# A state-space scan between attention and feed-forward: its pieces ordered anew on four engines

## What is computed

```python
dt = softplus(dt_unproj @ W_dt.T + b_dt)        # params = x @ W_params.T
u  = silu(causal_conv(x @ W_x.T))
A_tilde = exp(dt[..., None] * A);  B_tilde = (A_tilde - 1) / A
h = A_t * h + B_t * Bp_t[:, None, :] * u_t[:, :, None]   # 16 states for each feature
y_t = einsum('bn,bdn->bd', Cp_t, h)
y = (y + u * D_param) * silu(z);  return y @ W_out.T
```

## Time and profile before

| | |
|---|---|
| median of 3 runs | 1992.88 us (1989.69 to 1998.08) |
| profiled execution | 1992.94 us, span 1991.2 us, mean granted TensorE clock 0.970 |
| busy, page part 1 | PE 1885.0 us (95%), DVE 1611.4 (81%), ACT 1100.8 (55%), POOL 682.3 (34%) |
| the scan | 1208.2 to 1762.3 us |
| attention | 168 to 918 us |

### The profile page before, as it was taken

How to read it: one execution, slowest core, us unless ns; L and a number is a source line. 1 busy time by engine, 2 the same in 40 slices (tenths; PEclk the granted TensorE clock), 3 DMA queues, 4 the chain that set the end, 5 groups by cost and what they waited for, 6 DMA issues and landing times. The chain is left out here.

```text
span 1991.2 us, 26035 instructions
## 1 busy us (share of the span) xinstructions
PE 1885.0 (95%) x7526; PEld 845.0 (42%) x7526; DVE 1611.4 (81%) x2582; ACT 1100.8 (55%) x1526; POOL 682.3 (34%) x467
## 2 busy tenths in 40 slices
PE   8989999999999999999999997899999999699998
PEld 4532332332322323324676663343344344256666
DVE  6888998998999989985556658999998999954655
ACT  5643666665666666673234345776578558333322
POOL 3651000110100000010000017999999999800000
PEclk9997999998999999999999998999999999899999
DMA  4661222221221222204210023545444555400000
GB/s 136 163 155 33 44 44 45 44 49 39 49 44 44 49 44 44 44 12 143 65 43 32 11 56 102 135 136 143 143 132 124 135 129 164 94 6 16 22 21 22
DMA packets 100426, 147.14 MB, mean 74 GB/s; under 512 B 15120, under 2 KB 54432, under 8 KB 98752
## 3 DMA queue, kind: packets, MB, share of 16 engines
q1 hardware_dynamic: 100288, 145.42, 28.7%
HBM read 114.69 MB, written 30.29 MB: 73 GB/s over the span
## 5 line engine op out<-in xcount | busy, mean ns | idle before, releaser
L888 DVE TENSOR_REDUCE mx<-max_bank 128x1 f32<-128x512 f32 x976 | 627.9, 686 | 61.0 <-PE max_bank L791 59.9
L874 ACT ACTIVATE probs<-score_bank 128x1024 f32<-128x1024 f32 x512 | 496.7, 1021 | 277.0 <-PE score_bank L805 276.2
L791 PE MATMUL max_bank<-ks,qs 96*128 96x512 bf16 x976 | 338.9, 388 | 0.0
L805 PE MATMUL score_bank<-qs,ks 99*128 99x512 bf16 x1024 | 311.9, 386 | 12.9 <-issue 9.9
L1672 POOL TENSOR_TENSOR ring<-u,bc 128x1024 f32<-128x1024 f32 x128 | 301.2, 2367 | 0.0
L1744 PE MATMUL ys_bank<-outs,rec_diag 128*128 128x512 f32 x512 | 249.3, 616 | 46.2 <-POOL outs L1680 22.1
L858 PE MATMUL o_bank<-probs,vg 128*32 128x512 f32 x2048 | 273.6, 606 | 0.1
L1680 POOL TENSOR_TENSOR outs<-ring,bc 128x1024 f32<-128x1024 f32 x95 | 224.4, 2362 | 26.6 <-DVE ring L2024 26.3
L1312 PE MATMUL y_bank_f<-wpr_f,hid_f 128*128 128x256 f32 x992 | 229.9, 379 | 0.0
L1912 ACT ACTIVATE a_bank<-dt,decay_s 128x512 f32<-128x512 f32 x256 | 169.4, 684 | 109.1 <-DVE ring L2024 64.9
L745 POOL CAST neg_parts<-neg_max 16x128 bf16<-16x128 f32 x31 | 8.7, 281 | 639.8 <-DVE neg_max L901 639.8
(11 more groups left out here) (256 smaller groups left out, 2043.5 us busy)
## 6 DMA issues: line engine op xcount, KB each, us to landing
bc<-bc_scr SPq DMA_DIRECT2D x128, 512.0 KB, 4.9
qk_parts<-parts SPq DMA_DIRECT2D x128, 96.0 KB, 1.9
qs<-qk_parts SPq DMA_DIRECT2D x128, 64.0 KB, 4.2
o_scr<-o_sb SPq DMA_DIRECT2D x32, 256.0 KB, 2.1
ks<-qk_parts SPq DMA_DIRECT2D x16, 384.0 KB, 4.6
xn_s<-xn_scr SPq DMA_DIRECT2D x8, 515.0 KB, 6.3
x<-in_x_dram SPq DMA_DIRECT2D x8, 512.0 KB, 4.1
ks<-qk_parts SPq DMA_DIRECT2D x16, 256.0 KB, 3.7
```

Of the source, the lines that this page charges most:

```text
L791: nc.tensor.matmul(max_bank[(r + a) % MB][:], qs[r][0:SROWS, half, j, qt * P:(qt + 1) * P], ks[r][0:SROWS, j, kh * TW:(kh + 1) * TW], star ...
L805: mm = nc.tensor.matmul(score_bank[pair][:, j % 2], ks[r][0:MROWS, j, kt * P:(kt + 1) * P], qs[r][0:MROWS, qh, j, :], start=True, stop=True)
L874: nc.scalar.activation(probs[:, s % 2, 2 * pair:2 * pair + 2], score_bank[pair][:], ACT.Exp, scale=SOFTMAX_SCALE).then_inc(probs_ready, 1)
L888: nc.vector.tensor_reduce(mx[:, a // HU, a % HU:a % HU + 1], max_bank[(r + a) % MB][:], AX_X, ALU.max)\
```

## The change

In project, TensorE runs products whose result nobody reads (keep_warm) ahead of the row maxima: 4 before the first, 8 before the second, 2 before each further one. In merge_heads, SP issues the loads of tiles 3 and 4 of the heads before it fetches the reciprocals' parts. In the scan:

- ON_DVE is (0, 3, 6, 9, 12) instead of (3, 7, 11, 15) in tiles 0 to 6; tile 7 keeps its five.
- TensorE: parameters at n = 3; both outs of tile t-1 at n = 3 and 5 (before: of tile t-2 at n = 1 and 2); step sizes at n = 5 and 7 in different banks; all taps from n = 7 on; both add_terms at n = 12; both z halves at n = 14, in the last tile at n = 6 and 7; the next stage's first products before the last two sums.
- ScalarE: the two silus of u together at n = 13 and the two of z together at n = 1 of the next tile (n = 10 in the last tile), each pair between one load of the silu table and one back; exponential and logarithm over both halves in one instruction.
- VectorE: additions of tile t-1 at n = 5 and n = 7 (before: both of tile t-2 at n = 3).

```diff
--- before.py
+++ after.py
@@ -365,9 +365,22 @@
                 mm = nc.tensor.matmul(bias_bank[:, 0:D], bv_wide[:, c], wo[:, c], start=(c == 0), stop=(c == DC - 1))
             mm.then_inc(bias_made, 1)
+            def keep_warm(products):
+                for _ in range(products):
+                    nc.tensor.matmul(lat_bank[:], begun["qs0"][0:SROWS, 0, 0, 0:P], begun["ks0"][0:SROWS, 0, 0:TW],
+                                     start=True, stop=True)
+            pe.wait_ge(latent_kept, 2 * NT)
             pe.wait_ge(stack_in, 2 * STACK_LOAD)
+            keep_warm(4)
             for n in range(FIRST_PAIRS):
                 half, j, qt = n // (PAIRS // 2), n % (PAIRS // 2) // 4, n % 4
+                if n == 1:
+                    keep_warm(8)
+                elif n:
+                    keep_warm(2)
                 if n == 0:
                     pe.wait_ge(rotated, (NT - 1) * SIDES * ROTS + ROTS + 4)
                 elif n == 1:
@@ -1047,14 +1060,19 @@
             for h in range(2):
                 sp.wait_ge(o_out[h], 16 * B * NG + 16)
             sp.dma_start(sums[:], by_rows[HEADS0:, HD, :].rearrange("g (h t) -> g h t", h=PT)).then_inc(sums_in, 16)
+            sp.wait_ge(divided, DC)
+            load_heads(sp, by_rows, o_in, LOADED, heads_in[0])
             sp.wait_ge(recip_split, 5)
             sp.dma_start(recip_scr[:, HEADS0:].rearrange("s g (h t) -> (g h) s t", h=PT), recip_parts[:])\
                 .then_inc(recips_out, 16)
-            sp.wait_ge(recips_out, 16)
-            for part in range(3):
-                sp.dma_start(recip_heads[part * H:(part + 1) * H, B - 1], recip_scr[part, HEADS0:]).then_inc(recips_in, 16)
-            for t in range(LOADED, NT):
-
+            for t in range(LOADED + 1, NT):
+                if t == LOADED + 2:
+                    sp.wait_ge(recips_out, 16)
+                    for part in range(3):
+                        sp.dma_start(recip_heads[part * H:(part + 1) * H, B - 1], recip_scr[part, HEADS0:])\
+                            .then_inc(recips_in, 16)
                 sp.wait_ge(divided, DC * (t - LOADED) + DC)
                 load_heads(sp, by_rows, o_in, t, heads_in[t % LOADED])
             for dst, src in more_loads:
@@ -1567,12 +1585,13 @@
     RING = 6
     OUTS = 5
     AHEAD = 3
     LAG = 3
     D_UNIT = 8
-    ON_DVE, ON_DVE_LAST = (3, 7, 11, 15), (3, 6, 9, 12, 15)
+    ON_DVE, ON_DVE_LAST = (0, 3, 6, 9, 12), (3, 6, 9, 12, 15)
     with ExitStack() as ctx:
         m = Mem(nc, ctx)
         wz, wout, wtap, wpar, wdt, b_dt = (w[n] for n in ("wz", "wout", "wtap", "wpar", "wdt", "b_dt"))
@@ -1698,11 +1717,9 @@
             def parameters(t):
                 pe.wait_ge(xn_in[t % XN], 16 * (t // XN + 1))
-                if t > TPB:
-
-                    pe.wait_ge(x_new, 2 * (t - TPB) - 1)
-                elif t == TPB:
-                    pe.wait_ge(soft_made, DC * t)
+                if t > 1:
+                    pe.wait_ge(z_kept, DC * (t - 1))
                 product(w0[0:R + 2 * NS], [(wpar[:, c], xn_of(t, c)) for c in range(DC)], par_made)
             def u_taps(t, f, taps, bank):
@@ -1716,12 +1733,12 @@
             def step_size(t, f, bank):
                 product(bank, [(wdt[:, f * P:(f + 1) * P], par[0:R])], dt_made)
-            def add_terms(t, f):
+            def add_terms(t, f, bank):
                 pe.wait_ge(rest_made, 2 * t)
-                pe.wait_ge(split, SPLIT * t + 7 + f)
-                if f:
-                    pe.wait_ge(soft_made, DC * t + f)
-                product(w0[:], [(ident[:], part[:, f]) for part in (e_part, rest_part, log_part, relu_part)], terms_added)
+                pe.wait_ge(split, SPLIT * t + 8)
+                pe.wait_ge(u_kept, DC * t + f + 1)
+                product(bank, [(ident[:], part[:, f]) for part in (e_part, rest_part, log_part, relu_part)], terms_added)
             def z_half(t, f, bank):
                 product(bank, [(wz[:, c, f * P:(f + 1) * P], xn_of(t, c)) for c in range(DC)], z_made)
@@ -1754,62 +1771,55 @@
             for t in range(NT):
                 more = t + 1 < NT
                 for n in range(NS):
-                    if t >= TPB and n == 1:
-
-                        pe.wait_ge(soft_made, DC * (t + 1))
-                        out(t - 2, 0, w0)
-                    if t >= TPB and n == 2:
+                    if more and n == 3:
+                        parameters(t + 1)
+                    if t and n == 3:
                         pe.wait_ge(z_kept, DC * t)
-                        out(t - 2, 1, w1)
+                        out(t - 1, 0, w1)
+                    if more and n == 5:
+                        pe.wait_ge(par_kept, t + 2)
+                        step_size(t + 1, 0, w0[:])
+                    if t and n == 5:
+                        pe.wait_ge(x_new, 2 * t - 1)
+                        out(t - 1, 1, w1)
                     if more:
-                        if n == 4:
-                            parameters(t + 1)
-
-                            if t >= TPB:
-                                pe.wait_ge(x_new, DC * (t - 1))
-                            pe.wait_ge(z_kept, DC * t)
-                            u_taps(t + 1, 0, (0, 1), w1[:])
-                        if n == 5:
-                            u_taps(t + 1, 0, (2, 3), w1[:])
-                        if n == 6:
-
-                            pe.wait_ge(par_kept, t + 2)
-                            step_size(t + 1, 0, w0[:])
+                        if n == 7:
+                            if t:
+                                pe.wait_ge(x_new, 2 * t)
+                            step_size(t + 1, 1, w1[:])
+                            pe.wait_ge(split, SPLIT * (t + 1) + 2)
+                            u_taps(t + 1, 0, (0, 1), w0[:])
                         if n == 8:
-
-                            pe.wait_ge(split, SPLIT * (t + 1) + 2)
-                            step_size(t + 1, 1, w0[:])
+                            u_taps(t + 1, 0, (2, 3), w0[:])
                         if n == 9:
-                            pe.wait_ge(u_kept, DC * (t + 1) + 1)
+                            pe.wait_ge(split, SPLIT * (t + 1) + 4)
                             u_taps(t + 1, 1, (0, 1), w1[:])
                         if n == 10:
                             u_taps(t + 1, 1, (2, 3), w1[:])
                         if n == 12:
-                            add_terms(t + 1, 0)
+                            add_terms(t + 1, 0, w0[:])
+                            add_terms(t + 1, 1, w1[:])
                         if n == 14:
-                            add_terms(t + 1, 1)
-                    if n == 13:
-
-                        if more:
-                            pe.wait_ge(u_kept, DC * (t + 1) + DC)
-                        else:
-                            pe.wait_ge(norm.kept, DC)
-                        z_half(t, 0, w1[:])
-                    if n == 15:
-
-                        pe.wait_ge(z_kept, DC * t + 1)
+                            pe.wait_ge(soft_made, DC * (t + 1) + 1)
+                            z_half(t, 0, w0[:])
+                            pe.wait_ge(soft_made, DC * (t + 2))
+                            z_half(t, 1, w1[:])
+                    if not more and n == 6:
+                        z_half(t, 0, w0[:])
+                    if not more and n == 7:
+                        pe.wait_ge(x_new, 2 * t)
                         z_half(t, 1, w1[:])
-                    if not more and n == 5:
-
-                        pe.wait_ge(x_new, 2 * (t - 1))
-                        out(t - 1, 0, w0)
-                    if not more and n == 6:
-                        out(t - 1, 1, w1)
                     if not more and n == 10:
-                        pe.wait_ge(x_new, 2 * t)
+                        pe.wait_ge(z_kept, DC * t + DC)
                         norm.turn(nc, pe, 0, (w0, w1))
                     if t * NS + n >= LAG:
                         unit_sum(t * NS + n - LAG)
@@ -1820,15 +1830,16 @@
                 mm.then_inc(next_ready, 1)
             for g in range(UNITS - LAG, UNITS):
+                if g == UNITS - 2:
+                    pe.wait_ge(norm.kept, DC)
+                    pe.wait_ge(next_in, 16 * len(next_loads))
+                    pe.wait_ge(scanned, DC * (UNITS - 1))
+                    next_hidden(0)
+                    next_hidden(1)
                 unit_sum(g)
-            pe.wait_ge(norm.kept, DC)
-            pe.wait_ge(next_in, 16 * len(next_loads))
-
-            pe.wait_ge(scanned, DC * (UNITS - 1))
-            next_hidden(0)
             out(NT - 1, 0, w0)
             out(NT - 1, 1, w1)
-            next_hidden(1)
         @block.scalar
         def _(act):
@@ -1862,21 +1873,18 @@
             def soft_split(t, f, bank):
                 act.wait_ge(dt_made, DC * t + f + 1)
-                if t:
-
-                    act.wait_ge(soft_made, DC * t)
+                act.wait_ge(soft_made, DC * t)
```

(63 more changed lines are left out.)

## The result

The changed kernel takes 2014.68 us, the median of four runs (2011.09 to 2020.53); the kernel before took 1991.29 in four runs beside it (1986.09 to 1998.08). The ratio is 1.0111, with a 95% interval of 1.0082 to 1.0139: 23.4 us slower. The profiled execution is the slowest of the four (2020.53 us, span 2018.7), so its span lies 27.5 us above the 1991.2 of before, about 4 us more than the medians differ by.

The account below looks back on a forecast made before the run. The prediction took a loop through gating, VectorE's additions and TensorE's queue as the bound: 23.4 (six tiles) + 4.8 - 3 - 2.2 - 0.3 = 22.7 us on 1992.88, less two for the clock, gave 2014 us; range 1986 to 2034.

Parts of the forecast that it names:

- The loop: Scan tile: TensorE's 110 records (47.3 us) queue behind VectorE's second addition at 21.9 us and reach the next gating.
- The length of a tile: Scan, gating to gating: 70.4 us on average without clock loss, 71.3 with it, against 67.4 before.
- The clock's term: TensorE at half rate behind n = 7 in each scan tile: 0 to 3.4 us, taken as 0.9.
- Where TensorE idles: Scan tile, between gating and taps: about 4 us for the parameters' copy, 1.8 and 3.5 for the two additions.
- What VectorE would show: Scan: VectorE idle 5 to 7 us a tile, waiting for TensorE before weightings 12 or 0 and for dt decays.
- ScalarE's pieces: Scan tile: the logarithm delays a decay by 1.3 to 1.5 us; rest piece and paired silus add 0.3 to 1.2.
- rival (a): Scan: ScalarE's long pieces decide instead, 66.4 us a tile, 1982 us in all; chance 17%.
- The second leg: Scan: the taps wait for ScalarE's first split at n = 8, priced for tile 0 only.
- First tile: Scan tile 0: gating at about 1290 instead of 1285.5, as its taps wait for ScalarE's first split; +4.8 us.
- Last tile: End of scan: two additions less, one or two stalls less, next stage's products sooner; -3 us, between -5 and 0.
- Stages ahead of the scan: Fillers ahead of attention -2.2 us and the merge's earlier loads -0.3.
- the loads: Merge: loads come sooner, but TensorE shows no idle time there; -0.3 us, between -0.8 and +0.3.

Follow-up runs that it names:

- x1: Changed kernel with VectorE's additions at n = 3 and 4, TensorE's second out at n = 4, ScalarE's pieces one step earlier: 1970.81 us, tile 64.0.
- x2: Changed kernel with only VectorE's additions moved to n = 3 and 4 and TensorE's second out to n = 4, ScalarE unmoved: 2019.8 us, tile 71.55.
- x8: Changed kernel with the next stage's first products again behind the last sums: 71.5 us from gating 6 to the next stage's first product, after 73.6.
- x4: Kernel before with only the filler products ahead of attention and the merge's new order of loads: 1987.84 us, ratio 0.9966.
- x12: Kernel before with only the filler products ahead of attention, the merge's loads as before: 1986.98 us.
- x10: x1 with VectorE weighting states 3, 7, 11, 15 as in the kernel before: 1992.85 us, tile 67.59.
- x3: Changed kernel with the first half of each output computed three times and the second twice, on TensorE: 2013.04 us, tile 70.64.

## Why the prediction was right, point by point

**The loop decides: right.** TensorE starts the second step size 22.5 us after gating, where the working had it behind an addition at 21.9 (seen at 1595.71, 21.8). The queue behind it has no idle time until state 15. x1 takes the loop away and its whole cost goes.

**The length of a tile: 70.4 without the clock, 71.3 with it; measured 70.64 and 71.76.** The clock's term was 0.9 and is 1.1. The six tiles cost 26.3 us instead of 23.4, as the two terms were each 0.2 us a tile short.

**Where TensorE idles: the order right, the sizes too large.** Forecast were 4, 1.8 and 3.5 us for par and the two additions; tile 5 shows 3.99, 0.82 and 0.46, the six tiles on average 4.0, 0.7 and 1.2. The missing 3 us are the half-rate products (3.78 for 1.97, 4.79 for 3.60): they fill idle time, as the working said of them, and delay nothing there.

**What VectorE would show: right in its places, a little short in its size.** Forecast 5 to 7 us a tile, before the weightings of states 12 and 0 and before a scale of the next state 0; measured 7.4, at these places and before the scale of state 12. GpSimd idles 9.2 us a tile where 5 or more was forecast.

**ScalarE's pieces: the logarithm right, the rest not shown.** The working gave 1.3 to 1.5 us for the logarithm and 0.3 to 1.2 for the others, and from it rival (a)'s 66.4 us a tile. In the changed kernel VectorE waits 1.16 and 1.55 us by turns for the decay of state 12, right behind the logarithm's piece. ScalarE in tile 5, up to that decay:

```profile
1605.30 1.30 ACT L1920 ACTIVATE a_bank<-dt,decay_s 128x512 f32<-128x512 f32 x2 [2.30 <-DVE outs L2035]
1606.62 1.28 ACT L1885 ACT_TABLE_LOAD   x1
1607.91 1.15 ACT L1887 ACTIVATE log_part<-e_part,ones 128x1024 f32<-128x1024 f32 x1
1609.08 1.28 ACT L1870 ACT_TABLE_LOAD   x1
1610.38 1.30 ACT L1920 ACTIVATE a_bank<-dt,decay_s 128x512 f32<-128x512 f32 x2
```

In every tile of the six there is one, 1.35 us on average, as forecast. For the rest piece and the silus of u the six tiles show no wait. VectorE's 64.4 us of work and 1.35 are 65.7, so rival (a)'s 66.4 may have been some tenths too dear. No run shows it: x1 opens the loop, with a tile of 64.0, but has the pieces a step earlier, and x2, which leaves them in place, keeps the loop. What is shown is that the loop opened and the pieces earlier together measure 23 us below the kernel before, where the rival had 11.

**The second leg: missed.** ScalarE's split at n = 8 was counted for tile 0 alone. It stood behind the addition in every tile, so moving the additions alone bought nothing. It didn't change the sum of the changed kernel, since the other leg ended last there by about 1.4 us (taps 23.6 us after gating, in x2 22.2). The expectation of x2 had this leg, with the taps at 21.5 (seen: 22.2); what it lacked were the 1.8 us that the taps lose at half rate.

**First tile:** +4.8 forecast, +5.7 measured. **Last tile:** -3 forecast with bounds of -5 and 0, +1.1 measured, outside them and of the other sign. The step that failed is "the next stage's first products stand ahead of the last sums, so that the products after the last gating end sooner": the gating waits for those sums (6.48 us at 1783.83), and products put ahead of it delay it by more than they save behind it; x8 puts this at 2.2 us. With 71.5 us from gating 6 on, x8 is still 1.9 us above the forecast for this stretch, and which of its other terms (two additions less, one or two stalls less) failed stays open.

**Stages ahead of the scan:** -2.5 forecast, -5.5 in the profiled execution, of which 2.8 are the clock in the merge; x4's ratio gives 3.2 to 10.4 us. The term was too small, and how much of it is the fillers stays open. For the loads the prediction had nearly nothing, as TensorE showed no idle time there; that held because the slow first group covered them (x12).

**The sum:** 22.7, of which two were taken off, against 23.4 between the medians. Against the 27.5 us between the traces the working is 4.8 short: 2.9 in the six tiles, 0.9 in the first, 4.1 in the last, less 3.0 ahead of the scan. The last tile and the stages ahead of the scan missed in opposite ways, and the medians lie only 23.4 apart, since the profiled execution is 6 us above its own. The forecast of 2014 beside 2014.68 is in that part luck; the loop and its size are not.

## What to carry to other kernels

A step moved later in one engine's order is to be priced by what is queued behind its waiter: add the work behind the wait up to the next point where the engines meet, and compare with the period; here 22 + 47 us met a period of 67. When such a loop is opened, look for every wait that ends within a microsecond or two of the first, since moving one alone brings nothing (0.2 and 0.6 us a tile) where moving both brings 7.8. A change with real gains inside (a balanced set of weightings, paired table switches) can still measure slower than what it replaces; before it is dropped, look which single order keeps its gains from the end.

## What the runs showed of the hardware that was not expected

TensorE lost rate in a pattern that idle time alone doesn't foretell: after 2.21 us of idle time in x2 eight records of sums took 5.40 us instead of 3.60, while in the kernel before, after 2.41 and again 2.14 us of idle time in tile 2, the rows behind took 1.98 and 1.93 us, close to their full rate. The same sixteen products of the merge took 3.72, 5.26, 5.41 and 6.56 us in four traces (the changed kernel, x10, x12, x3).

Keeping TensorE busy with repeated products brought the granted clock of the tiles from 0.93 to between 0.98 and 1.00, and cost no time, as the products fell into idle time: TensorE's busy time rose from 65.4 to 67.2 us a tile and the tile became 1.1 us shorter.

VectorE runs without a gap that the trace shows for five tiles of x1 in a row, 320.7 us, while GpSimd works 62.0 to 62.8 us and TensorE 61.1 to 62.2 in each beside it; GpSimd's operation stays at 2.36 us and 2.31 from start to start whether VectorE takes four weightings or five.
